# A graph network kernel: target bins of 87 nodes in place of 81, 36 bins in 12 triples, 300 chunks in place of 325

## The reference

```
# L1: one message per edge from the source's row and the edge's own attributes
h = concat([x[row], edge_attr]);  h = relu(h @ W1a + b1a) @ W1b + b1b
ssum = segment_sum(h, col);  mean = ssum / max(count, 1)
# L2: eight relations, each with its own 64x64 matrix
for r in range(8):  out += segment_sum(where(edge_type == r, x[src] @ weight[r], 0), dst)
# L3: two weighted sums (positive and negative weights), twice
agg = segment_sum((x @ W.T)[src] * norm, tgt)          # layer 1 on x, layer 2 on its result
```

## Time and profile before

| | |
|---|---|
| median of 3 timed runs | 4437.56 us (4431.42 to 4444.34) |
| profiled execution | 4402.9 us, span 4401.2 us |
| busy in the span | TensorE 3083.2 us (70%), weight loads 2395.9 (54%), VectorE 3220.0 (73%), ScalarE 1438.3 (33%), GpSimd 1408.1 (32%) |
| mean granted TensorE clock | 0.866 of 2.4 GHz |
| edge pass ep | 2181 to 2675 us from the span's start |
| rp | 2832 to 3518 |
| sp | 3576 to 3913 |
| sq | 3970 to 4371 |

### The profile page before, as it was taken

One profiled execution on the slowest core, in us unless ns is written; L12 is line 12 of the kernel. 1 busy time (PEld: TensorE's weight loads), 2 busy tenths in 40 slices (PEclk: granted clock), 3 DMA queues, 4 the chain that ended last, 5 costly groups with the idle time before them and its releaser, 6 DMA issues. The chain is left out here.

```text
span 4401.2 us, 85012 instructions
## 1 busy us (share of the span) xinstructions
PE 3083.2 (70%) x29186; PEld 2395.9 (54%) x29186; DVE 3220.0 (73%) x7812; ACT 1438.3 (33%) x2737; POOL 1408.1 (32%) x1203
## 2 busy tenths in 40 slices
PE   0077777787228338338499996588888769968996
PEld 0044554454102102112299995278888759958996
DVE  7766666666389799789577774277777679977887
ACT  0034444444115125125299992233333200000000
POOL 0055555555254464464000000166666300000000
PEclk9988888888569669669699996599999979989998
DMA  8844555545458448458366660111111023313332
GB/s 319 339 129 133 164 149 157 160 132 154 141 168 260 143 136 265 125 162 262 108 216 220 217 207 15 66 23 25 24 24 24 17 66 109 107 41 100 91 90 56
DMA packets 414245, 587.75 MB, mean 134 GB/s; under 512 B 76564, under 2 KB 302443, under 8 KB 413445
## 3 DMA queue, kind: packets, MB, share of 16 engines
q1 hardware_dynamic: 366293, 448.13, 33.9%
q0 software_dynamic: 37888, 67.18, 5.4%
q10 hardware_dynamic: 9648, 67.01, 3.7%
HBM read 340.53 MB, written 235.00 MB: 131 GB/s over the span
## 5 line engine op out<-in xcount | busy, mean ns | idle before, releaser
L848 POOL DMA_INDIRECT slots<-bc_rec,idx x496 | 485.6, 979 | 390.4 <-ACT bc_rec L808 275.3
L1108 PE MATMUL psum<-a_probs,z 128*65 128x512 f32 (+1 forms) x1050 | 448.2, 561 | 141.9 <-DVE a_probs L1041 141.8
L1344 DVE TENSOR_SCALAR rp_hot_src<-rp_key_rows,lane 128x384 bf16<-128x384 f16 x1560 | 382.2, 315 | 175.6 <-issue 80.8
L1577 PE MATMUL psum<-rel_pieces,rp_hot_src 128*128 128x192 bf16 x4680 | 438.7, 248 | 72.6 <-issue 55.6
L1306 POOL DMA_INDIRECT rp_rows<-rel_rows,slot_rel x390 | 410.8, 1053 | 224.0 <-issue 86.5
L1076 ACT ACTIVATE a_tops<-a_tops,a_s_low 128x1024 f32<-128x1024 f32 (+2 forms) x300 | 284.0, 947 | 568.6 <-DVE a_tops L1032 568.3
L484 POOL DMA_INDIRECT slots<-h,idx x192 | 328.9, 1713 | 353.5 <-DMA h<-recs 305.1
L1577 PEld LDWEIGHTS psum<-rel_pieces,rp_hot_src 128*128 128x128 bf16 x4680 | 386.0, 99 | 96.8 <-issue 74.7
L1108 PEld LDWEIGHTS psum<-a_probs,z 128*65 128x65 f32 x1050 | 122.2, 138 | 468.4 <-DVE a_probs L1041 296.6
L704 DVE TENSOR_SCALAR bc_first_t<-bc_ramp,bc_key_t 128x128 f16<-128x128 f16 x500 | 135.3, 271 | 306.0 <-PE psum L730 175.4
L1032 DVE SCALAR_TENSOR_TENSOR a_tops<-table,a_s_rest,big 128x1024 f32<-128x1024 f32 (+2 forms) x300 | 306.9, 1023 | 32.0 <-DMA big<-shift_rows 31.8
(11 more groups left out here) (459 smaller groups left out, 6697.1 us busy)
## 6 DMA issues: line engine op xcount, KB each, us to landing
a_counts<-edge_counts SPq DMA_DIRECT2D x150, 512.0 KB
slots<-big ACTq DMA_DIRECT2D x65, 1005.0 KB
ep_rec<-slots SPq DMA_DIRECT2D x65, 1005.0 KB, 7.5
edge_counts<-bc_counts SPq DMA_DIRECT2D x12, 3125.0 KB
hot_rows<-ep_hot_src SPq DMA_DIRECT2D x325, 96.0 KB, 4.6
sp_hot_src<-hot_rows SPq DMA_DIRECT2D x325, 96.0 KB, 2.1
sq_hot_src<-hot_rows SPq DMA_DIRECT2D x325, 96.0 KB, 2.0
a_counts<-edge_counts SPq DMA_DIRECT2D x75, 282.5 KB
```

Of the source, the lines that this page charges most:

```text
L848: pool.indirect_dma_start(k.slots, bass.IndirectOffsetOnAxis(k.idx[:, first + t:first + t + 1], 0), rec[:, j, t, :], None).then_inc(scatte ...
L1108: last = nc.tensor.matmul(sums[:, a:b], k.z[:, s, 0:D + 1], probs[:, a:b], start=s == 0, stop=True, skip_group_check=True)
L1344: last = v.tensor_scalar(hot_src[:, n % HOT_SLOTS, rel, :], key_rows[:, n % 2, :], k.lane[:, rel:rel + 1], None, ALU.is_equal)
L1577: last = nc.tensor.matmul(to, hot_src[:, n % HOT_SLOTS, r, s * P:(s + 1) * P], pieces[:, row, r, :], start=s != 1 and r == 0, stop=True, s ...
```

## The change

One constant: `SPAN` goes from 81 to 87. From it follow `BINS` (39 to 36), `NTRIPLE` (13 to 12), `NCHUNK` (325 to 300), the number of slots, `BIN_ROWS` (84 to 90), the fill DMAs (65 to 60), the parts in which a pass's sums are placed (63 to 60), and how many edges don't find room in the 128 slots of their group.

```diff
 CAP = P
 SLOTS = 3
-SPAN = 81
+SPAN = 87
 BINS = -(-N // SPAN)
 NTRIPLE = BINS // SLOTS
 NCHUNK = NTRIPLE * NT
```

## The result

The changed kernel took 4372.82 us (median of 4, 4358.1 to 4380.47) beside 4440.95 for the kernel before (median of 4, 4431.42 to 4447.77): ratio 0.9838, 95% interval 0.9819 to 0.9856, which is 72 us less (64 to 80). The forecast was 4371 us, 66.5 less. The pair of profiles shows only 22.5 us of it (span 4378.7 against 4401.2).

The account below looks back on a forecast made before the run. ScalarE and TensorE bound the edge-message pass, hand-overs the relation pass, VectorE and TensorE the near pass, TensorE the far pass. 137.3 - 13.8 - 62 + 5 = 66.5 us less, 4437.6 to 4371 us; 8-in-10 range 4345 to 4402.

Parts of the forecast that it names:

- One triple less per pass: Four edge passes: 325 chunks become 300, saving 35.3 + 48.3 + 24.4 + 29.3 = 137.3 us.
- Wider bins: Remaining 300 chunks: longer target one-hots on VectorE and weight loads on TensorE cost 1.5 + 0.7 + 5.6 + 6 = 13.8 us.
- if sp's doesn't grow: Near pass: sign that the forecast is wrong, VectorE not being its bound; 5.6 us of growth was expected.
- The 1.5 in sq: Far pass: only the first of six adding weight loads per chunk shows, 5 ns x 300 = 1.5 us.
- rp's 6: Relation pass: wider one-hot and loads cost between 0 and 12 us; 6 taken.
- Second turns: Left-over-edge loop at each pass's end turns twice instead of once: 54.0 us plus clock loss, 62 taken.
- Half clock: Second turns: some 4 us of matmuls run at half speed, losing 2 us per pass, 8 in all.
- Fill: Slot table filling near the start: five of 65 fills go, saving between 0 and 8 us; 5 taken.
- Weight loads on the path: Rival, adding matmuls in the passes: longer loads all show, costing 39 instead of 13.8 us, time 4396; chance 0.12.
- A starving turn: Rival, left-over loop: TensorE trickles after the jump back, 109 us more, time 4480; chance 0.04.
- a third tile: Rival, left-over loop: over 256 left edges add another 62 us, time 4433; chance 0.03 with anything else.
- The starving stretch: Rival, relation pass start: TensorE's 19 us loss moves with code; gone 4352 (chance 0.11), doubled 4390 (0.06).

Follow-up runs that it names:

- the later runs: Both kernels timed again unchanged, on one chip with the follow-ups: kernel before 4129.85 us (ratio 1.000), changed kernel 4072.0 us (ratio 0.9858 to the kernel before).

## Why the prediction was right, and where it wasn't

- *One triple less per pass, 137.3 us.* With 84 or 90 rows ep, sp and sq repeat within 0.2 us per triple in every profile. rp's 48.3 was so in the profile that the forecast was made from; in the later runs it is 41.2 to 42.2, and the term 131. Right, with a size that belongs to its surroundings.
- *Wider bins, 13.8.* Measured alone: 8 to 22 us by 325 chunks, and by the profiles about 0.5 (rp) + 0.1 (sp) + 0.1 (sq) us per triple, some 9 by 12 triples. A third of what 102 rows cost is 6 us. So the term of 13.8 was too large by some 5 to 8 us, though the 8 to 22 holds it; the step that failed is "in sp VectorE goes from one operation to the next without idling, so all of it counts: 5.6 us". By that sign of its own ("if sp's doesn't grow") the forecast was all but wrong here: sp's triple grew by 0.11 to 0.17 us where 0.47 was expected, 1.3 to 2.1 us in all. The one-hot alone brought none of it; it came with the loads. The 1.5 in sq (one load in six shows) was right at both widths, 0.12 and 0.37 us per triple. rp's 6 was a guess between 0 and 12, and came out at 6 by the means, known no better than to a few us.
- *Second turns, 62.* 59.1 and 59.5 in the two profiles of the change, 64.5 alone. Half clock was put at 8 us; the 75 matmuls of the second turns took 6.03, 3.63, 6.12 and 7.18 us in place of 4.4, 2.4, 4.4 and 4.4 in the first profile, 7.3 more.
- *Fill, 5.* 7.2 at the start of the counting stage; not to be told in the time.
- *What the sum left out.* The longer wait for the last triple's placement, 8.9 us in the first pair of profiles and 6.2 in the later one. The forecast put it at nothing without a reason.
- *Sum.* With the measured sizes: 137.3 - 6 to 9 (width) - 59 to 65 (turns) - 9 (placement) + 7 (fill) = 61 to 70 less, where 64 to 80 was measured; in the later runs, with 131 for the triples and 6 for the placement, 58 to 67, where 48 to 69 was measured. The large terms, the triples and the turns, were right. That 66.5 came so near is in part luck: a width term some 5 to 8 us too large stood in for a placement term of 6 to 9 that was missing.
- *Rivals.* Weight loads on the path fell by sq's triple (29.40, not 30), and at 102 columns (0.37, not 2.3 us). A starving turn fell by 59.1, and a third tile by two turns in every pass. The starving stretch did not go or double with the code: it was there in both first profiles, before and after, and gone in the later ones, with either code. The pair of profiles was 45 us short of the timed difference; 19.6 us of it lie in the counting stage and 18 in rp's triples, the two places in which the same program was seen to vary, so scatter of this kind is the likely reason. What makes instructions late in some executions and not in others stays open; no experiment tried it.

## What to carry to other kernels

Before a "full" engine is taken as the bound, add up its records of one chunk: where they exceed the chunk's time they overlap, and a dose on that engine alone (a wider operation whose extra output nobody reads) settles it in one run. Coarser groups that save chunks send work into the overflow path; price that path by its chain of hand-overs, and shorten the chain first, for here that raised the worth of this change from about 60 to 88 us. Look also at what waits for the last group's results: here nothing hid the wait for them. Size a change by time ratios from one chip and by the stages that repeat, not by the difference of two profiled spans.

## What was not expected of the hardware

One program took 4441 us in the first runs and 4130 in the later ones, ratio 0.93, with nearly all of it in two stages: 871 against 697 us in the counting stage, and 48.3 against 42.0 per triple in rp. The DMA queues moved the same bytes (587.75 MB). Waits for "issue" differed in both: in the counting stage ScalarE had 133.7 us of them at line 793 in the first profile and none in the new one. The granted clock was 1.00 in rp in both profiles, and 0.84 against 0.95 in the counting stage. Whether the lower clock there is a cause or only follows from TensorE's waits, no run shows. And a VectorE operation 57 ns longer by its own record let the next one start at the same time as before.
